# Issuing the next block's layer-norm chain after the query, key and value products of a transformer layer

## What is computed

```python
x = x + attn(layernorm(x))      # q, k, v = y @ Wq, y @ Wk, y @ Wv; scores = q k^T / 32
                                # softmax over axis 1, the query axis; out[j] = sum_i attn[i, j] v[i]
x = x + ffn(layernorm(x))       # silu(y Wg^T) * (y Wu^T), then Wd^T; int weights / 127, hidden 3072
```

## Time and profile before

| | us |
|---|---|
| median of 2 runs | 2074.54 |
| the two runs | 2064.92, 2084.15 |
| the profiled execution | 2064.14 |
| its span, slowest core (core 5) | 2062.6 |
| spans of the 8 cores | 2048.9 to 2062.6 |
| PE busy | 1861.5 (90% of the span) |
| DVE busy / ACT busy | 547.1 (27%) / 390.2 (19%) |
| PE's idle time before the L522 matmuls, put down to a q_f cast | 35.3 |

### The profile page before, as it was taken

How to read it: one execution, slowest core, us unless ns; L and a number is a source line. 1 busy time by engine, 2 the same in 40 slices (tenths; PEclk the granted TensorE clock), 3 DMA queues, 4 the chain that set the end, 5 groups by cost and what they waited for, 6 DMA issues and landing times.

```text
span 2062.6 us, 23419 instructions; the slowest of 8 cores (2048.9 to 2062.6 us)
## 1 busy us (share of the span) xinstructions
PE 1861.5 (90%) x9216; PEld 868.0 (42%) x9216; DVE 547.1 (27%) x794; ACT 390.2 (19%) x583; POOL 58.3 (3%) x112
## 2 busy tenths in 40 slices
PE   3999969896489999997379999999999999999999
PEld 1444424343144444443234444444444444444444
DVE  1344322332134433332222221222213222112211
ACT  6210112225541022323011100111001110011100
POOL 2000000000100001110000000000000000000000
PEclk9999989898699999999589999999999999999999
DMA  9632289985731026662942232322322222212112
GB/s 202 97 70 31 33 131 147 160 190 152 221 106 36 1 59 177 183 176 82 305 154 82 82 103 92 133 82 82 102 93 82 82 82 103 92 51 82 62 56 88
DMA packets 167500, 223.86 MB, mean 109 GB/s; under 512 B 81824, under 2 KB 130976, under 8 KB 166816
## 3 DMA queue, kind: packets, MB, share of 16 engines
q1 hardware_dynamic: 157408, 178.32, 29.0%
q0 software_dynamic: 9984, 44.05, 12.1%
HBM read 176.19 MB, written 71.30 MB: 120 GB/s over the span
## 4 chain that ended last, share of the span: by engine, by line
PE 77%; DMA 15%; DVE 2%; SPq 2%; issue 2%; ACT 1%; POOL 0%; DVEq 0%; another core or an unknown queue 0%; ACTq 0%; POOLq 0%
PE P_S L983 31%; PE P_ATT L1067 16%; PE P_S L522 14%; PE P_ATT L704 7%; PE P_S L602 6%; DMA out<-x1st 5%; DMA stage<-wg_bf 3%; DMA x1ln<-out 2%; SPq L91 2%; DMA wk_sb<-wk 2%; DMA wg_bfT<-stage 2%; PE P_ATT L522 1%; PE P_PT L675 1%; DVE x1st L722 1%; ACT junk_s L381 1%
## 5 line engine op out<-in xcount | busy, mean ns | idle before, releaser
L983 PE MATMUL P_S<-y,wut 128*128 128x512 bf16 x1536 | 366.2, 382 | 34.3 <-DVE hh L1013 34.3
L983 PE MATMUL P_S<-y,wgt 128*128 128x512 bf16 x1536 | 364.3, 380 | 0.0
L1067 PE MATMUL P_ATT<-wdt,hh 128*128 128x512 bf16 x1536 | 332.2, 379 | 0.9 <-DVE hh L1013 0.9
L1001 ACT ACTIVATE sg<-P_S 128x512 bf16<-128x512 f32 x192 | 114.7, 597 | 849.0 <-PE P_S L983 806.7
L1013 DVE SCALAR_TENSOR_TENSOR hh<-P_S,sg 128x512 bf16<-128x512 f32 x192 | 132.5, 692 | 513.8 <-PE P_S L983 513.8
L704 PE MATMUL P_ATT<-v_t,pt_sb 128*128 128x512 bf16 x1024 | 230.5, 384 | 35.6 <-DVE pt_sb L686 35.6
L983 PEld LDWEIGHTS P_S<-y,wut 128*128 128x128 bf16 x1536 | 150.7, 98 | 218.2 <-issue 39.0
L602 PE MATMUL P_S<-q_f,k_f 128*128 128x512 bf16 x1024 | 228.1, 381 | 1.9 <-DVE k_f L532 1.9
L983 PEld LDWEIGHTS P_S<-y,wgt 128*128 128x128 bf16 x1536 | 150.8, 98 | 182.7 <-issue 3.0
L1067 PEld LDWEIGHTS P_ATT<-wdt,hh 128*128 128x128 bf16 x1536 | 150.1, 98 | 181.7 <-issue 1.4
L704 PEld LDWEIGHTS P_ATT<-v_t,pt_sb 128*128 128x128 bf16 x1024 | 100.7, 99 | 160.5 <-issue 43.8
(11 more groups left out here) (60 smaller groups left out, 738.7 us busy)
## 6 DMA issues: line engine op xcount, KB each, us to landing
xpool<-x SPq DMA_DIRECT2D x68, 512.0 KB, 6.5
wgt<-wg_bfT SPq DMA_DIRECT2D x24, 1024.0 KB, 5.0
wut<-wu_bfT SPq DMA_DIRECT2D x24, 1024.0 KB, 6.6
out<-x1st SPq DMA_DIRECT2D x32, 512.0 KB, 3.8
x1ln<-out SPq DMA_DIRECT2D x32, 512.0 KB, 8.7
x1res<-out SPq DMA_DIRECT2D x32, 512.0 KB, 4.6
out<-outst SPq DMA_DIRECT2D x32, 512.0 KB, 2.9
wg_bf<-wg POOLq DMA_DIRECT2D x4, 1536.0 KB, 17.2
```

Source lines behind the costliest of these rows:

```text
L983: e.matmul(P_S[:, slot_i * 512:(slot_i + 1) * 512], wbuf[:, p * 4096 + dc * 512 + hcc * 128: p * 4096 + dc * 512 + hcc * 128 + 128], y2[:, ...
L1001: e.activation(sg[:, p2 * 512:(p2 + 1) * 512], P_S[:, g_slot * 512:(g_slot + 1) * 512], AF.Silu, scale=INV127), inc="ACT")
L1067: e.matmul(P_ATT[:, asl * 512:(asl + 1) * 512], hh[:, hc * 1024 + th * 512 + toff: hc * 1024 + th * 512 + toff + 128], wdt[:, hc * 1024 + ...
```

## The change

The call of `emit_ln_chain(s, ib + 1)` moves from ahead of the q matmuls of block ib to behind its v matmuls. No instruction is added or removed.

```diff
@@ phase_a(s), in the loop over ib
                     if s == 1 and ib == 1:
                         emit_sqrt_batch(0)
-                    if ib + 1 < 4:
-                        emit_ln_chain(s, ib + 1)
                     pl.wait("tensor", "DVE", ev_max)
                     pl.wait("tensor", *w_ready["q"])
                     for ec in range(EC):
@@ ... the q, k and v groups stand here ...
                                 v_t[:, o:o + 512], sl_vt, [sl_wv, sl_y1],
                                 att_banks=(ib == 3))
+                    if ib + 1 < 4:
+                        emit_ln_chain(s, ib + 1)
```

## The result

The changed kernel takes 1.0091 times the time of the kernel before, with a 95% interval of 1.006 to 1.0123: 19 us more, between 12 and 25. Its profiled execution took 2080.6 us against 2064.1. The median over all its executions is 2101.92 us (before: 2067.12), because executions in which a die is granted a lower clock are among them; the ratio leaves those out.

The account below looks back on a forecast made before the run. PE was taken as the busiest engine, with three waits for q_f casts totalling 35.3 us in phase_a. Gains of 31.3 us less losses of 44.4 gave net +13.1, or 2077; forecast 2080 us, own range 2072 to 2092, wide 2061 to 2098.

Parts of the forecast that it names:

- the base: Time before the change: profiled 2064.1 us, two timed runs with median 10.4 us above it; forecast put a little above the sum.
- Only DVE's order changes: In phase_a, six chains move behind their block's 24 casts on DVE; other engines' lists keep their order.
- Gain 1: Block (1, 0): PE resumes its q matmuls at about 534.5 instead of 553.04, 18.5 us; a 9.2 us wait stays.
- Gain 2: Block (1, 1): the 5.29 us wait goes and the next 32 matmuls save 1.28 us, together 6.6 us.
- Gain 3: Block (0, 0): a 2.26 us wait goes and the weights wk and wv land earlier, 6.2 us (0 to 8.0).
- The steps: Six steps between blocks: each loses 5.7 us of exposed chain and 1.7 us of clock, 7.4 us; together 44.4 us.
- The sum: Whole kernel: gains 31.3 us, losses 44.4 us, net +13.1 us.
- Statistics in time: Blocks of phase_a: load and statistics take some 20 us against 41.4 us of matmuls, so no cost.
- That the clock holds: Rival: at the steps between blocks the clock stays up, each costs 5.2 us; no change, 2064 us; chance 13%.
- That the weights do not land earlier: Rival: in block (0, 0) gain 3 is 0 and v starts at 69.11 as before; 2083 us; chance 12%.
- Other collisions in `phase_b(0)`: Rival: transfers there collide differently, one PE wait more or less; 2066 to 2095 us; chance 12%.

Follow-up runs that it names:

- the two runs without it: Unused second issue of the chain of block (1, 0) left out: of the changed kernel, ratio 1.0032; of the kernel before, one execution, 2055.3 us.
- the chain between k and v: Kernel before, with the next block's chain issued between the k and v products in both sequences; ratio 0.9859 (0.9771 to 0.9947).
- the filled kernel: Changed kernel plus 23 extra matmuls with unused results on PE in each of the six steps between blocks; ratio 1.0001 (0.9949 to 1.0053).
- the run with sequence 0 alone: Kernel before, with the chain moved behind the v products only in sequence 0; ratio 1.0072 (1.0026 to 1.0118).

## Why the prediction was right, and where its terms were off

The forecast was 16 us more than the profiled execution before, out of a sum of 13; measured were 16.5 us in the profiled executions and 19 us by the ratio. That 16 and 16.5 agree so closely is in part luck: 3 of the 16 us were put on for the base and not for any mechanism, and the slowest core had a long `phase_b(0)`. On the mean of the cores the span grew by 12.0 us, to be compared with the sum of 13.1. The reasons given hold, step by step:

- **Only DVE's order changes, and the waits move from the casts to the chain.** Shown: one wait for q_f is left of three, and at the six steps the releaser of PE is ya.
- **Gain 1, predicted 18.5 us.** Over the cores the wait in block (1, 0) went from 26.4 to 6.5 us, 19.9; by the stretches it is 19.2 (13.6 us less, and 5.6 us of exposed chain that the stretch now contains). The wait that stays was expected at 9.2 us: the statistics of the second chain end 11.6 us after the first q matmul on core 2 and not 14.0 as in the earlier trace rows; why was not looked for. That the second chain would be the one that stays was read from the earlier trace rows and is shown by the two runs without it.
- **Gain 2, predicted 6.6 us.** The wait of 5.29 us is gone in every core. With the chain between k and v, where nothing is paid for it, the stretch is 90.6 us instead of 98.1: 7.5 us on the mean of the cores.
- **Gain 3, predicted 6.2 us, is the term that was mis-sized: about 4.5 us** (5.6 us of exposed chain less the 1.1 us by which block (0, 0) grew). Core 5, from which the rows came, in the changed kernel:

```profile
49.49 13.97 PE L522 MATMUL P_S<-y,wk_sb 128*128 128x512 bf16 x64 [1.69 <-DMA wk_sb<-wk]
63.30 13.98 PE L522 MATMUL P_S<-wv_sb,y 128*128 128x512 bf16 x64
```

  k was expected at 49.1 and v at 62.9, and core 5 comes close. But its q also begins 0.7 us earlier than in the kernel before, so the time from its first q to its last v matmul falls by 5.1 us (51.45 to 46.34) and not by 6.2. On the mean of the cores it falls by 4.5, with k at 50.2 and v at 64.9. The v start is 2.0 us late in two parts. First, wk lands later than reckoned: 1.1 us. Second, the sum lets k run 13.8 us straight behind a wait for wk, with no term for the clock, although show 64 k matmuls of 15.66 us behind such a wait of 2.01 us. On five cores PE now waits 3.6 to 5.0 us for wk, and on four of these the k matmuls take 15.4 to 16.5 us: 0.9 us on the mean. On core 5 the clock stayed up. So two steps were off: the 2.7 us of service that wk was to get back, and the clock behind the wait that is left, which was put at nothing. One core's rows couldn't show how much both vary.
- **The steps, predicted 7.4 us each.** Measured 7.4 in sequence 0. The split was off: 5.1 and 2.3 instead of 5.7 and 1.7, because the 0.5 us by which slow transposes lengthen the exposed chain is clock too. The 5.2 us that the prediction gave for a clock that holds is what the filled kernel shows, 5.1.
- **The sum.** Gain 3 was 1.7 us too high, gains 1 and 2 were 0.7 and 0.9 too low. That the three add up to 31.2 against the predicted 31.3 is luck.
- **Statistics in time, predicted at no cost.** Shown: at all six steps, on all eight cores, the mean follows the last v cast without a wait for ACT's statistics.
- **Rivals.** That the clock holds is refuted by the changed kernel's own stretches. That the weights do not land earlier is refuted. Other collisions in `phase_b(0)` gave some of the difference between 13 and 16.5: the slowest core of the changed kernel is core 2, whose stretch (0, 3) to (1, 0) is 347.3 us against a mean of 339.2. It isn't shown that the change has a part in it, and the run with sequence 0 alone speaks against it.

The rule of the Trainium skill that was weighed (TensorE: Matmul & The Clock Gate, on oscillation: each long enough wait in a loop pays for the fall of the clock anew) is borne out here: the changed kernel pays at all six steps, and the filled kernel, without the wait, at none. The other one (DMA: Bandwidth & Descriptors, queues drained in turn) agrees with the queue shares: 72.7% and 32.5% side by side in the kernel before, 106.6% for the weights when no x load is queued.

What the change was to bring is there, about 31 us of waits, clock and transfers; it was given back, and more, at the steps. The kernel with the chain between k and v keeps the gain.

## To carry to other kernels

A chain of small operations with a wait in it has two deadlines in an in-order list: it must not stand ahead of work that feeds the bounding engine before its own inputs are there, and not so late that its result is due when it starts. Count both from the profile, the time when the inputs are ready and the length of the chain up to its consumer, and put it in between; at either end it costs. When a wait goes, look at what else stands in the same place of the list: the unused second chain cost little until the first wait was gone. And a short idle time of TensorE ahead of dense matmuls is to be counted with what the clock takes behind it: here 2.3 us for 3.8 us of idle time.

## What the hardware showed beyond that

Extra work made the changed kernel faster, 1.0001 (0.9949 to 1.0053) against 1.0091 (1.006 to 1.0123) times the kernel before: in each of the six steps the 23 matmuls that compute nothing take about 5 us and lie wholly in time in which PE stood still, and the granted clock stays up.

In the kernel with the chain between k and v, cores 6 and 7 ran sequence 1 at a granted clock that is neither 0.5 nor 1.0. Stretches of core 6:

```profile
529.50:546.30 16.80, 16.80 (x66) 6.96 (x65) 5.54 (x8) 8.44 (x16) 2.16 (x4) 0.81 0.77 179
546.30:563.00 16.70, 16.70 (x65) 6.95 (x64) 6.29 (x14) 4.84 (x5) 1.08 (x2) 0.81 0.70 200
693.00:713.00 20.00, 19.06 (x89) 8.48 (x88) 5.78 (x9) 0.00 (x0) 0.00 (x0) 1.00 0.00 1
```

64 matmuls take 17.0 us there, on the other cores 13.98; cores 4 and 5, of the same die, have 1.00 in the same three stretches. The Trainium skill (TensorE: Matmul & The Clock Gate, the note on the peak-current limiter) names such a clock, 13/16 of full speed, and advises to expect it whenever all cores run dense matmuls. The value agrees with the 0.81 here; the advice does not: all eight cores run the same dense matmuls, and most of their stretches in these profiles have a granted clock of 1.00. What starts and ends it was not tried.
